# Cross-attention and a dense mixture of attention experts: QKV groups of 512 columns on 24 slots instead of 384 on 32

## What is computed

```
h   = layernorm(x)
rw  = gate(h)                                     # [rows, 16]
q   = einsum('bte,bted->btd', rw, einsum('btc,ecd->bted', h, q_proj))   # k and v alike
att = softmax(causal(q @ k.T / 8)) @ v            # [rows, 64]
x   = x + einsum('bted,edc->btc', att[:, :, None, :] * rw[..., None], o_proj)
```

## Time and profile before

| | |
|---|---|
| median of 3 runs | 1070.73 us (1070.47 to 1071.62) |
| span of the profiled execution | 1066.4 us; the page gives no other time of it |
| PE busy | 996.7 us, 93% |
| PE weight loads busy | 875.1 us, 82% |
| DVE busy | 611.1 us, 57% |
| ACT, POOL busy | 239.7 us, 22%; 257.6 us, 24% |
| mean granted TensorE clock | 0.960 |

### The profile page before, as it was taken

The page is one execution under the profiler, slowest core; times in us unless marked ns, Lnnn a source line. Parts: engine busy times, 40 slices in busy tenths (PEclk is TensorE's granted clock), DMA queues, the critical chain, the costliest instruction groups (busy, mean ns, idle before and its releaser), DMA issues.

```text
span 1066.4 us, 16692 instructions
## 1 busy us (share of the span) xinstructions
PE 996.7 (93%) x5320; PEld 875.1 (82%) x5320; DVE 611.1 (57%) x1843; ACT 239.7 (22%) x575; POOL 257.6 (24%) x408
## 2 busy tenths in 40 slices
PE   5778676999999999999999999999999999999987
PEld 3455446998989898988898899889998999999975
DVE  7787845764646465555555555555564746464631
ACT  5666641221111111111111111111121202120201
POOL 4644426312121202120212121202020303030201
PEclk8898877999999999999999999999999999999997
DMA  4545422300101010101010101010101010101010
GB/s 165 192 146 202 142 93 70 98 11 10 51 11 50 10 50 11 50 11 50 1 59 0 60 0 59 0 60 0 59 0 50 10 49 10 49 12 42 8 33 27
DMA packets 30576, 53.71 MB, mean 50 GB/s; under 512 B 7241, under 2 KB 7241, under 8 KB 30386
## 3 DMA queue, kind: packets, MB, share of 16 engines
q1 hardware_dynamic: 30514, 53.01, 14.6%
HBM read 36.22 MB, written 16.78 MB: 50 GB/s over the span
## 4 chain that ended last, share of the span: by engine, by line
PE 79%; issue 2%; POOL 1%; DVE 1%; POOLq 0%; DMA 0%; DVEq 0%; ACT 0%
PE psQ L1275 50%; PE psO L1367 16%; PE psM L1333 3%; PE psT L1318 2%; PE psM L1352 2%; PE psT L1247 1%; PE psT L1236 1%; PE psT L1290 1%; PE psM L1336 1%; PE psT L1299 1%; PE psQ L1367 1%; POOL probs L913 0%; PE psT L1307 0%; PE psT L1255 0%; DMA mixed_f<-in_w_o 0%
## 5 line engine op out<-in xcount | busy, mean ns | idle before, releaser
L1275 PE MATMUL psQ<-Wqkv_hi,hT_hi 128*128 128x384 f32 x1024 | 364.2, 356 | 0.0
L1275 PE MATMUL psQ<-Wqkv_lo,hT_hi 128*128 128x384 f32 x1024 | 348.4, 340 | 0.0
L1275 PE MATMUL psQ<-Wqkv_hi,hT_lo 128*128 128x384 f32 x1024 | 347.9, 340 | 0.0
L1143 DVE SCALAR_TENSOR_TENSOR acc<-psQ,RW,acc 128x192 f32<-128x192 f32 x448 | 166.1, 413 | 301.9 <-PE psQ L1275 271.4
L1275 PEld LDWEIGHTS psQ<-Wqkv_hi,hT_hi 128*128 128x128 f32 x1024 | 193.6, 189 | 16.3 <-issue 3.5
L1275 PEld LDWEIGHTS psQ<-Wqkv_lo,hT_hi 128*128 128x128 f32 x1024 | 194.1, 190 | 1.8
L1275 PEld LDWEIGHTS psQ<-Wqkv_hi,hT_lo 128*128 128x128 f32 x1024 | 193.6, 189 | 0.0
L948 POOL TENSOR_TENSOR mixedT_lo<-mixed_f,mixedT_hi 128x512 fp32r<-128x512 f32 x64 | 81.7, 1285 | 187.7 <-ACT mixedT_hi L1020 187.7
L1367 PE MATMUL psO<-Wo_hi,mixedT_hi 128*128 128x512 f32 x248 | 100.1, 404 | 1.8 <-POOL mixedT_lo L948 1.8
L1367 PE MATMUL psO<-Wo_hi,mixedT_lo 128*128 128x512 f32 x248 | 97.5, 393 | 0.0
L1367 PE MATMUL psO<-Wo_lo,mixedT_hi 128*128 128x512 f32 x248 | 97.1, 392 | 0.0
(11 more groups left out here) (182 smaller groups left out, 1395.0 us busy)
## 6 DMA issues: line engine op xcount, KB each, us to landing
X<-in_x SPq DMA_DIRECT2D x8, 1024.0 KB, 5.6
x_scratch<-XR SPq DMA_DIRECT2D x16, 512.0 KB, 2.9
X<-x_scratch SPq DMA_DIRECT2D x32, 256.0 KB, 2.7
resid<-x_scratch SPq DMA_DIRECT2D x32, 256.0 KB, 3.2
out<-resid SPq DMA_DIRECT2D x32, 256.0 KB, 2.1
stage<-in_w_qkv SPq DMA_DIRECT2D x8, 768.0 KB, 6.1
mixed_f<-in_w_o SPq DMA_DIRECT2D x8, 256.0 KB, 3.3
CTX<-in_ctx_in SPq DMA_DIRECT2D x8, 154.0 KB
```

Source lines behind the costliest of these rows:

```text
L1143: dve.scalar_tensor_tensor(out=acc[e][:], in0=src, scalar=w, in1=acc[e][:], op0=ALU.mult, op1=ALU.add).then_inc(expert_added, 1)
L1275: last = pe.matmul(psQ[g % 4][:, 0:PW], x[:, c * P:(c + 1) * P], w[:, c, g * PW:(g + 1) * PW], start=(c == 0 and m == 0), stop=(c == KC - ...
```

## The change

A QKV group has 512 columns, so a tile has six groups instead of eight and a batch 24 slots instead of 32. A group no longer ends with an expert: `pieces_of` cuts it at the experts' borders, and DVE adds 3 or 4 pieces of 64 to 192 columns a group, 20 a tile. All tables are new and turned round: each gives for a job its slot, 24 and above meaning the next batch's slot less 24 (`due`). Statistics are computed at the end of a tile (g = 5) for the tile after the next one, and H at the head of the next tile (g = 0), now ahead of DVE's additions of that slot.

```diff
-QK_T_AT = {12: 0, 16: 1, 28: 2, 0: 3}
-SCORES_AT = {16: 0, 18: 1, 29: 2, 2: 3}
-PROBS_T_AT = {18: 0, 20: 1, 31: 2, 4: 3}
-GATES_T_AT = {21: 0, 5: 1}
-MIX_AT = {23: (0, 0), 24: (0, 1), 25: (0, 2), 26: (0, 3),
-          7: (1, 0), 8: (1, 1), 9: (1, 2), 10: (1, 3)}
-PROJECT_AT = {27: [(0, 0)], 28: [(0, 1)], 30: [(1, 0), (1, 1)],
-              11: [(2, 0)], 12: [(2, 1)], 14: [(3, 0), (3, 1)]}
-Y_AT = {29: 0, 31: 1, 13: 2, 15: 3}
-STATS_SLOT, NORM_SLOT, H_T_SLOT, LOGITS_SLOT = 0, 1, 3, 4
-LOGITS_T_SLOT = 5
+QK_T_AT = {0: 9, 1: 12, 2: 19, 3: 24}
+SCORES_AT = {0: 10, 1: 13, 2: 21, 3: 25}
+PROBS_T_AT = {0: 12, 1: 14, 2: 22, 3: 26}
+GATES_T_AT = {0: 15, 1: 27}
+MIX_AT = {(h, u): 16 + 12 * h + u for h in range(2) for u in range(4)}
+PROJECT_AT = {(0, 0): 19, (0, 1): 21, (1, 0): 22, (1, 1): 22,
+              (2, 0): 31, (2, 1): 33, (3, 0): 34, (3, 1): 34}
+Y_AT = {0: 22, 1: 23, 2: 34, 3: 35}
+NORM_SLOT, H_T_SLOT, LOGITS_SLOT, STATS_SLOT = 0, 1, 2, 5
+LOGITS_T_SLOT = 3
...
+def pieces_of(g, width):
+    found, at = [], g * WIDE
+    while at < (g + 1) * WIDE:
+        e, c = divmod(at, width)
+        n = min(width - c, (g + 1) * WIDE - at)
+        found.append((e, slice(c, c + n), slice(at - g * WIDE, at - g * WIDE + n)))
+        at += n
+    return found
...
+    def due(table, k, b, qkv, lead):
+        return [(item, b - at // SLOTS) for item, at in table.items()
+                if at % SLOTS == k and (lead if at >= SLOTS else qkv)]
...
                 pool.wait_ge(stats_ready, t + 1)
+                if not isinstance(t, int) or t >= 1:
+                    pool.wait_ge(norm_done, t)
...
             row_stats(0)
             normalise(0, 0)
+            row_stats(1)
             lo(hT[0][1][:], slice(0, D), hT[0][0][:])
...
+                    if prepare and g == NORM_SLOT:
+                        normalise(t + 1, 1 - tp)
                     if qkv:
                         dve.wait_ge(qkv_summed, SLOTS * b + k + 1)
...
-                        for e in range(2):
-                            src = psQ[g % 4][:, e * Q3:(e + 1) * Q3]
+                        for n, (e, cols, at) in enumerate(PIECES[g]):
+                            src, sums = psQ[k % 4][:, at], acc[e % 2][:, cols]
...
-                    if prepare and g == NORM_SLOT:
-                        normalise(t + 1, 1 - tp)
...
-                    if prepare and g == STATS_SLOT:
-                        row_stats(t + 1)
+                    if qkv and (prep or j < TILES - 2) and g == STATS_SLOT:
+                        row_stats(t + 2)
...
-                                last = pe.matmul(psQ[g % 4][:, 0:PW], x[:, c * P:(c + 1) * P],
-                                                 w[:, c, g * PW:(g + 1) * PW],
+                                last = pe.matmul(psQ[k % 4][:], x[:, c * P:(c + 1) * P],
+                                                 w[:, c, g * WIDE:(g + 1) * WIDE],
```

More of the change, by code:

```diff
@@ L92, in cross_attention_then_experts_kernel @@
     Q3 = 3 * DH
[L93 to L94 removed]
+    SLOTS = TILES * GROUPS
     OC = E * DH // P
@@ L897, in _ @@
             powers(0, 0)
+            powers(1, 1)
             done = 1
@@ L985, in body @@
                                        ).then_inc(wo_hi, 1)
-                    if attn and k in PROBS_T_AT:
-                        i = PROBS_T_AT[k]
+                    for i, ab in due(PROBS_T_AT, k, b, qkv, lead):
                         n = moves.step()
@@ L1011, in body @@
                                        ).then_inc(moved_hi, 1)
-                    if attn and k in MIX_AT:
-                        h, u = MIX_AT[k]
+                    for (h, u), ab in due(MIX_AT, k, b, qkv, lead):
                         act.wait_ge(moved_lo, moves.step())
@@ L1023, in body @@
                         copy_logits()
-                    if attn and k in SCORES_AT:
-                        i = SCORES_AT[k]
+                    for i, ab in due(SCORES_AT, k, b, qkv, lead):
                         act.wait_ge(neg_max_ready, TILES * ab + i + 1)
@@ L1293, in body @@
                         probs_moved[i] = moves.now()
-                    i = tile_copies(k, qkv, lead)
-                    if i is not None:
-                        bank = next_bank(nat_ready, TILES * (b - 1 if k == 0 else b) + i + 1)
+                    for i, bt in due(QK_T_AT, k, b, qkv, lead):
+                        bank = next_bank(nat_ready, TILES * bt + i + 1)
                         for s in range(2):
@@ L1302, in body @@
                         qk_moved[i] = moves.now()
-                    if attn and k in GATES_T_AT:
-                        h = GATES_T_AT[k]
+                    for h, ab in due(GATES_T_AT, k, b, qkv, lead):
                         bank = next_bank(gates_divided, TILES * ab + 2 * h + 2)
@@ L1338, in body @@
                         last.then_inc(scored, 1)
-                    if attn and k in VALUES_AT:
-                        h = VALUES_AT[k]
+                    for h, ab in due(VALUES_AT, k, b, qkv, lead):
                         pe.wait_ge(exp_done, TILES * ab + 2 * h + 2)
@@ L1357, in body @@
                         logits = sum_logits(1 - tp, h_moved)
-                    for i, part in PROJECT_AT.get(k, []) if attn else []:
+                    for (i, part), ab in due(PROJECT_AT, k, b, qkv, lead):
                         a = TILES * ab + i
```

118 lines of the change are left out of this document (53 added, 65 removed).

## The result

The median went from 1071.06 to 1149.49 us (1145.09 to 1150.9 in four runs), a ratio of 1.0739, 95% interval 1.0717 to 1.0762: **7.4% slower, 78.4 us**, where 52 were forecast. The profiled execution took 1149.88 us, its span is 1148.2 (1066.4 before), its mean granted clock 0.944 (0.960 before). The time lies above the 1095 to 1145 us that the sum's own bounds gave, and half a microsecond inside the end of the wide range, 1150.

A forecast was written before the change was run, and what follows sets the result against it. PE's matmul stream bounds the second block, every new wait adding in full. -19.8 stream, -5.6 entries, +57.3 waits, +5.8 turns, 0 start and end, +14 clock: +52 on 1070.7 gives 1123 us, own range 1095 to 1145, wide range 1080 to 1150.

The forecast's parts named there:

- The QKV stream: PE's QKV matmuls: 3072 of 384 columns at 0.177 us become 2304 of 512 at 0.2275, saving 19.8 us.
- The rival at 8 in 100: 512-wide QKV matmuls run no better by the column than 0.235 us each: 1140 us, 8 in 100.
- The rival of the clock: The clock falls oftener, as many falls again and more, PE idling six times a batch: 1150 us, 17 in 100.
- Fewer entries: QKV matmuls coming behind another kind: 7 fewer a batch, at 0.1 us each, saving 5.6 us.
- Waits 1 and 2: Projections at slots 22 and 10' wait for DVE's residual at the output bank: 1.75 and 1.2 us, +14.0 and +8.4.
- Slot 19: PE waits for QKT2's bank after mix 2, then mix 3's bank after hT_lo: 0.44 + 1.46 us, +13.3 in all.
- Slot 7': PE waits for mix 3's bank, then for mixedT_lo behind POOL's powers: 0.44 + 0.71 us, +8.0 in all.
- Slot 13: Scores of tile 1 wait for qkT_lo, its transpose now one slot ahead: 1.0 us, eight times, +8.0.
- The turn: At four loop turns PE waits 2.6 us for H, then 0.8 for qkT_lo; less 4.8 that go, +5.8.
- The clock: Falls to 1.2 GHz after PE's new waits, one per 4.8 us of waits, two thirds counted: +14 us.
- Start and end: One more DMA, statistics and powers first (+2), H of tile 1 earlier (-2 to -4): 0, +-4.
- The signs named for being wrong: A loop batch without a turn taking under 110 us, or PE not waiting for resid, would refute the forecast.

The follow-up runs named there:

- e5: e3 with tile 2's QK transposes one slot later, at slot 20 instead of 19: 1061.26 us, 0.9927 of the kernel before.
- e12: e5 with 32 bytes of padding ahead of Wqkv and 96 behind, so Wqkv, Wo, hT and mixedT all lie at 32 modulo 128: 1048.95 us, 0.9812.
- e6: e5 with tile 1's first statistics behind tile 0's hT_lo instead of ahead of it: 1060.67 us, 0.9916.
- e2: The changed kernel with the statistics one slot earlier (g = 4 instead of 5): 1109.35 us, 1.0362 of the kernel before.
- e9: e5 with 32 bytes of padding ahead of Wqkv and 32 behind: Wqkv at 32 modulo 128, Wo, hT, mixedT at 96; 1054.32 us, 0.9861.
- e10: e5 with 32 bytes of padding ahead of Wqkv only: Wqkv at 32 modulo 128, Wo, hT, mixedT at 64; 1060.39 us, one run.
- e11: The kernel before, with 32 bytes of padding ahead of Wqkv and 32 behind: 1059.7 us, 0.9918.
- e3: The changed kernel with projections and residuals of tiles 1 and 3 one slot later and statistics one slot earlier: 1069.44 us, 0.9992 of the kernel before.
- e4: The kernel before with residuals of tiles 0 and 2 moved into the slot of the projection that waits for them: 1112.09 us, 1.0382.

## Why the forecast was wrong in size

The direction, the mechanism and nearly all its places held; what failed above all is one term of the sum, the price of a 512-wide QKV matmul. Set against e5, the same work with no loop wait, the time divides (from the start of tile 0's QK transposes of one batch to the next, in spans):

| term | forecast | measured |
|---|---|---|
| QKV stream and entries | -25.4 | -6.3 |
| waits, turns included | +67.9 | about +71 |
| clock in the batches | +14 | about +17 |
| the waits of the kernel before and their fall of the clock, which go | -4.8 | -6.6 |
| start and end | 0 | +6.2 |
| in all | +52 | +81.7 |

(The span grew by 81.7, the median by 78.4; the difference is within what single executions vary by. The prediction put 4.3 us around the span; in the runs on record it is 1.6 to 1.9, so that the profiled execution of the kernel before took some 1068.1 us, 3 below the median. This does not touch the forecast, which adds to the median.)

- **The QKV stream failed.** "The nearest row for that width is the output projection: 24 in 5.46 us, 0.2275 each." The width was the same, but not the operands' placement: the QKV group runs at 0.2335. A batch without waits went from 108.79 to 108.28 us, not to 105.6. Of a batch, the psQ matmuls took 70.57 us before (384) and 69.35 in e5 (288), 1.2 less, and the rest took 0.7 more, H's sixteen transposes 2.11 instead of 1.42 us. Together with the entries this is 19 of the 30 us missed: in the batches the stream itself saves some 4 us where 19.8 were forecast, and the 0.7 us a batch of the rest, 5.5 in all, stood in the sum at nothing. The -6.3 is 4.1 for eight batches and some 2 in the last batch's slots, whose cause was not looked for. The rival at 8 in 100 had this step right, but for another reason: the 0.235 of its run of 12 has the entry in it. The first matmul there takes 0.29 us to the next start and the other eleven 0.231 each:

```profile
635.66 0.45 PE L1367 MATMUL psO<-Wo_hi,mixedT_hi 128*128 128x512 f32 x1
635.95 0.39 PE L1367 MATMUL psO<-Wo_lo,mixedT_hi 128*128 128x512 f32 x1
...
638.49 0.34 PE L1275 MATMUL psQ<-Wqkv_hi,hT_hi 128*128 128x384 f32 x1
```

So that 0.235 is close to 0.2335 was luck. The rival of the clock named 1150 us, the number nearest to the measured one, but for 28 us more of falls, of which some 3 came. With the operands placed alike (e12) the wide groups run at 0.2275 as forecast, and a batch is 2.0 us below.
- **Fewer entries.** 24 entries in e5; the change has the 22 counted. An entry costs 0.292 us at 512 columns and 0.244 at 384: above the spacing 0.06 and 0.07, not 0.1, since some entries cost nothing above it. 29 x 0.067 - 24 x 0.058 = 0.55 us a batch, 4.4 in all where 5.6 were forecast, inside the -6.3.
- **Waits 1 and 2.** Forecast 1.75 and 1.2; idle before the first matmul 1.78 and 1.08. Start to start it is up to 0.3 more, since four pieces took 1.20 us, not 1.06, and the hand-over to PE 0.10.
- **Slot 19.** Two waits, start to start 0.82 and 1.79, forecast 0.44 and 1.46. **Slot 7'**: 0.53 for mixed_f and 0.99 for mixedT_lo, forecast 0.44 and 0.71. **Slot 1'**: qkT_lo 0.87, forecast 0.8.
- **Slot 13.** The place was right and the waiter wrong: H's transposes wait for the bank that probsT_lo still holds (0.85 idle, 1.24 start to start, forecast 1.0), and the scores behind them then hardly wait. I had looked at that slot for scores only.
- **The sum of them** in the last window above, which has neither turn nor fall: 116.50 - 108.28 = 8.2 us, forecast 7.8 (the six waits as listed). Over all batches 88.5 us lie above e5's; less 17 for the clock, 71 are left.
- **The turn.** H waits up to 1.5 us (1.9 start to start), not 2.6. Yet a turn costs 2.6 us as forecast (122.0, less 2.9 for two stretches at the lower clock, less 116.5): in these batches the waits at slot 7' are longer too, 0.7 and 0.9 us of idle time against 0.3 and 0.7 in the last window. The sum was right, its parts were not.
- **The clock.** Turn batches with 6.8 and 10.2 us at the 1.2 GHz level took 122.0 and 123.4 us, batches without a turn with 0 and 3.4 took 116.5 and 118.0: 1.4 to 1.5 us for 3.4 us at that level (1.6 forecast). Some 41 us of the six loop batches lie there, 12 such stretches: 17 us, forecast 14.
- **Start and end.** +3.6 and +2.6. Two of the first stand in e5 too and are not from waits of the loop; e6 speaks against the place of tile 1's statistics. From the first QKV matmul to tile 0's QK transposes 11.1 us lie at 1.2 GHz, 6.9 before and 9.0 in e5 (granted clock 0.86, 0.90 and 0.88), which at the price above is about half of the 3.6. At the end 20.5 us instead of 13.7 are at the lower clock. Why the clock is lower there, and what else makes the start longer, stays open.
- **The signs named for being wrong** did not show: no loop batch is under 110 us, and PE does wait for resid. Of what was to show in the profile, PE's busy share did fall below 90%, to 89%; the QKV spacing of 0.2275 and the waits of 2.6 us for H did not show.

## What to carry to other kernels

A stream rate is taken over from another group of instructions only with its operands' addresses beside it: here 128 bytes of padding are worth 12 us, more than the 8 us by which e5, the wide groups without waits, is ahead of the kernel before.

Where an order is packed anew, list for each slot the shared single things (a PSUM bank, a bank pair, a buffer) with the jobs that want them in that slot: an addition and the projection that overwrites its source in one slot, or three jobs on two banks, each cost 1.1 to 1.8 us every time, and the statistics just ahead of H made four later jobs late (e2). Put the statistics a slot ahead of the tile's end, and a projection of 5.5 us between that end and H's transposes: then the long chain through another engine, and even the loop's turn, are hidden.

## What the runs showed of the hardware

- **Operand placement.** fp32r matmuls of 128 x 512 with their weight loads start 0.2275 us apart where moving and stationary operands lie alike modulo 128 bytes, 0.230 if alike modulo 64 only (e9), 0.2335 if 32 bytes off (e5, e10); at 384 columns 0.177 if 32 bytes off and 0.173 if alike modulo 64 only (e11).
- **A part beside the columns that no placement tried removes.** At best 0.227 us for 512 columns (e12) is some 14 ns above 512 / 2.4 GHz. The Trainium skill (TensorE: Matmul & The Clock Gate, section Back-to-back issue gap) gives 2.5 ns for an isolated matmul; no run here comes near that. The matmuls here are a stream, with a weight load each, and the prediction set the figure against such a stream too.
- **Waits and the clock.** In the profiled execution e3 has a wait of 1.3 us in every loop batch and in none of them a stretch at 1.2 GHz; the change, with eight waits a batch, has one to three in five of six batches. In the kernel before a single wait of 1.14 us was followed by one, so a lone wait can do it, but did not in e3. e4, with two bank waits a batch, has one or two in five of six.

```profile
764.30:771.10 6.80, 6.80 (x17) 4.77 (x17) 2.18 (x6) 0.78 (x2) 0.00 (x0) 0.50 0.28 99
```

This window of the change shows one of the longer ones, 6.80 us at 0.50, 1.2 GHz: PE is busy throughout, but gets through 17 matmuls. Those of 512 columns start 0.427 us apart in it, which is 512 / 1.2 GHz, against 0.2335 at 2.4 GHz.
